# Third edge stage of a four-layer graph network: rows picked from the raw node features in two bfloat16 blocks, 176 columns, with ScalarE making 4 of 25 node blocks

## The reference, cut to what matters

```
q = x @ Wq + bq;  k = x @ Wk + bk;  v = x @ Wv + bv        # [3125, 64], 4 heads of 16
score = exp(clip(sum_over_16(k[src] * q[dst]) / 8, -5, 5))   # per edge and head
wv = segment_sum(v[src] * score, dst);  z = segment_sum(score, dst)
o = (wv / (z + 1)) @ Wo + bo;  h = x @ Wf + bf + o;  out = h + norm(h) * gamma + beta
```

## Time and profile before

| | us |
|---|---|
| median of 3 runs | 5953.28 (5952.83 to 5963.26) |
| span of the profiled execution | 5023.8 |
| time outside the span (5953.3 - 5023.8) | 929.5 |
| third edge stage, 3037 to about 3873 | 836 |
| first and second edge stage, about | 1000 and 1680 |

### The profile page before, as it was taken

One profiled execution on the slowest core, in us unless ns is written; L12 is line 12 of the kernel. 1 busy time (PEld: TensorE's weight loads), 2 busy tenths in 40 slices (PEclk: granted clock), 3 DMA queues, 4 the chain that ended last, 5 costly groups with the idle time before them and its releaser, 6 DMA issues. The chain is left out here.

```text
span 5023.8 us, 55747 instructions
## 1 busy us (share of the span) xinstructions
PE 3828.8 (76%) x16477; PEld 2687.1 (53%) x16477; DVE 4001.3 (80%) x5661; ACT 2076.3 (41%) x3728; POOL 3704.0 (74%) x3415
## 2 busy tenths in 40 slices
PE   1677777762999999999999947888883666677651
PEld 1344444432888888888888843333331443333321
DVE  3788888874899999999999856899996657677763
ACT  0577777751344444444444423444443322222221
POOL 6777777764788888888888637777776567777774
PEclk6899999985999999999999957899996778888875
DMA  8777887764788888888888643444443662222221
GB/s 304 261 274 277 283 282 281 281 213 141 281 326 316 320 322 317 325 314 328 316 320 323 250 93 111 131 131 131 132 129 99 240 248 66 72 68 72 66 62 44
DMA packets 359919, 1074.05 MB, mean 214 GB/s; under 512 B 101414, under 2 KB 124642, under 8 KB 315300
## 3 DMA queue, kind: packets, MB, share of 16 engines
q1 hardware_dynamic: 240788, 850.33, 44.9%
q0 software_dynamic: 103232, 158.19, 12.5%
q10 hardware_dynamic: 15696, 63.31, 3.1%
HBM read 677.98 MB, written 392.57 MB: 213 GB/s over the span
## 5 line engine op out<-in xcount | busy, mean ns | idle before, releaser
L1859 PE MATMUL COLS<-CF,XF 128*128 128x256 f32 x6272 | 1485.6, 380 | 6.2 <-DVE XF L1967 6.2
L1859 PEld LDWEIGHTS COLS<-CF,XF 128*128 128x128 f32 x6272 | 1135.0, 190 | 130.4 <-DVE XF L1967 6.6
L1135 ACT ACTIVATE OUT<-SC 128x576 f32<-128x576 f32 (+3 forms) x392 | 576.9, 1472 | 1082.2 <-DVE SC L1070 722.1
L1826 POOL DMA_INDIRECT G<-x_tab,SRC x784 | 835.7, 1066 | 229.1 <-issue 216.4
L1018 POOL DMA_INDIRECT G<-xl_tab,SRC x752 | 728.3, 969 | 229.2 <-issue 223.4
L1018 POOL DMA_INDIRECT G<-rel_tab,REL x672 | 641.5, 955 | 205.0 <-issue 205.0
L1018 POOL DMA_INDIRECT G<-kv_tab,SRC x640 | 628.6, 982 | 195.0 <-issue 193.5
L1444 PE MATMUL PICK<-HOT,KV 125*128 125x512 bf16 x2700 | 629.2, 397 | 132.4 <-ACT TURNED L1476 117.8
L1608 PE MATMUL MADE<-XM,W 128*128 128x512 f32 x896 | 484.6, 699 | 163.7 <-DVE XM L1696 163.6
L1444 PEld LDWEIGHTS PICK<-HOT,KV 125*128 125x128 bf16 x2700 | 272.2, 101 | 482.6 <-issue 179.6
L1262 PE MATMUL WK<-W,HT 128*128 128x256 f32 x1568 | 443.8, 409 | 0.0
(11 more groups left out here) (307 smaller groups left out, 6763.3 us busy)
## 6 DMA issues: line engine op xcount, KB each, us to landing
SHB<-ea9t SPq DMA_DIRECT2D x196, 1024.0 KB, 9.6
wkv_tab<-WKV SPq DMA_DIRECT2D x98, 1024.0 KB, 6.1
WKV<-wkv_tab SPq DMA_DIRECT2D x98, 1024.0 KB, 5.9
scan<-OUT SPq DMA_DIRECT2D x196, 288.0 KB
scan<-OUT ACTq DMA_DIRECT2D x98, 576.0 KB
rel_tab<-YS SPq DMA_DIRECT2D x50, 1024.0 KB, 12.6
RAW<-spread SPq DMA_DIRECT2D x196, 256.0 KB, 2.8
spread_q<-ZQ SPq DMA_DIRECT2D x98, 512.0 KB
```

The source lines that it names most:

```text
L1135: nc.scalar.activation(self.OUT[d][:, :, 0:WD], SC[b][:, 0:WD, 1:1 + C].rearrange("p r j -> p j r"), ACT.Copy).then_inc(self.copied_out, 1)
L1826: pool.indirect_dma_start(out=e.G[0][b][:, col, :], out_offset=None, in_=x1_tab, in_offset=bass.IndirectOffsetOnAxis(ap=SRC[:, at:at + 1], ...
L1859: nc.tensor.matmul(acc, XF[b][:, k, edges_], CF[:, k, :], start=(k == 0), stop=False)
```

## The change

Instead of the rows of `k` and `v`, the raw node features `x` are picked, and are projected after that.

- `X3` takes the place of `KV3`: two bfloat16 blocks of 128 columns instead of three. Block 0 holds the high and the middle part of the 64 features side by side, block 1 the low part and 64 zeros. PE makes 100 matmuls a batch instead of 150.
- The sum isn't transposed back but multiplied by `WKV2` (the weights of `k` and `v`, one above the other, so that the parts are added), with the biases first, in two halves of four columns (`project_half`).
- Chunks 8 to 95 each have 2 picked columns: 22 batches of four chunks, 176 columns instead of 144. POOL gathers 608 columns instead of 640.
- DVE makes 21 of the 25 blocks of `HOT` (in quarters of 6, 5, 5 and 5), in 462 compares instead of 450. ACT makes the other 4 in three parts, as relu(1 - |source - node|): an `Abs` for each block and a `Relu` for each part. These lie between `place` and `OUT` of the first three chunks of four; `take` lies in the fourth.
- The sources are loaded and narrowed one batch earlier, and ACT makes the first batch's 4 blocks before chunk 0.

```diff
+PERIOD = 4
+BATCHES = (NCH - PICK_FROM) // PERIOD
 def picks(t):
-    return 0 if t < PICK_FROM else (2, 1, 2, 1, 2)[(t - PICK_FROM) % 5]
+    return 2 if PICK_FROM <= t < PICK_FROM + PERIOD * BATCHES else 0
...
-                            act.wait_ge(m_copied, len(units))
-                            nc.scalar.activation(KV3[:, :, 0, :], TAB[:, :, 0:128], ACT.Copy).then_inc(kv_high, 1)
+                            nc.scalar.activation(X3[:, :, 0, 0:64], X[:, :, :], ACT.Copy).then_inc(x_high, 1)
...
+                            nc.gpsimd.memset(X3[:, :, 1, 64:128], 0.0).then_inc(blank, 1)
...
+                QUARTERS = [range(0, 6), range(6, 11), range(11, 16), range(16, 21)]
+                BY_ACT = [(21, 22), (23,), (24,)]
...
+                        def pick_rows(k, first, last):
+                            for piece in range(2):
+                                for half in range(2):
+                                    edges_ = slice(512 * half, 512 * half + 512)
+                                    ins = nc.tensor.matmul(PICK[:, edges_], X3[N, k, piece, :], HOT[N, k, edges_],
+                                                           start=(first and piece == 0), stop=(last and piece == 1))
+                            return ins
+                        def pick_by_act(i):
+                            wait(pe, act_compared, 3 * i + 3)
+                            wait(pe, taken, i)
+                            for k in range(21, K):
+                                ins = pick_rows(k, k == 21, False)
+                            ins.then_inc(act_read, 1)
...
+                        def project_half(i, h):
                             wait(pe, taken, i + 1)
-                            wait(pe, placed, 5 * i)
-                            for q in range(8):
-                                ins = nc.tensor.transpose(BACK[:, q * P:(q + 1) * P], TURNED[:, q * P:(q + 1) * P],
-                                                          IDENT[:, :])
+                            wait(pe, placed, 4 * (i - 1) + 2 * h + 2)
+                            nc.tensor.matmul(BACK[:, 512 * h:512 * h + 512], IDENT[:, :],
+                                             vec("bk", 2).unsqueeze(1).to_broadcast([P, 4, P]), start=True, stop=False)
+                            for q in range(4 * h, 4 * h + 4):
+                                ins = nc.tensor.matmul(BACK[:, q * P:(q + 1) * P], TURNED[:, q * P:(q + 1) * P],
+                                                       WKV2[:, :], start=False, stop=(q == 4 * h + 3))
                             ins.then_inc(turned_back, 1)
...
+                        def compare_by_act(i, part):
+                            ks = BY_ACT[part]
+                            if part == 0:
+                                wait(act, narrowed, i + 1)
+                                wait(act, act_read, i)
+                            wait(act, act_compared, 3 * i + part)
+                            for a, k in enumerate(ks):
+                                nc.scalar.activation(AWAY[N, a, :], ID16[i % 2][N, :], ACT.Abs,
+                                                     bias=MINUS_NODE[N, k - 21:k - 20]).then_inc(away, 1)
+                            wait(act, away, 4 * i + (2, 3, 4)[part])
+                            nc.scalar.activation(HOT[N, ks[0]:ks[-1] + 1, :], AWAY[N, 0:len(ks), :], ACT.Relu,
+                                                 bias=ONES[N, 0:1], scale=-1.0).then_inc(act_compared, 1)
...
-                            if t % 5 == 0 and 1 <= t // 5 <= BATCHES:
-                                take(t // 5 - 1)
+                            if t % PERIOD == 3 and t // PERIOD < BATCHES:
+                                take(t // PERIOD)
+                            elif t % PERIOD != 3 and t // PERIOD + 1 < BATCHES:
+                                compare_by_act(t // PERIOD + 1, t % PERIOD)
                             e.store_rows(act, t, n, b, t < 4)
```

More of the change, by code:

```diff
@@ L1414, in _ @@
                         load_sources(0)
+                        load_sources(1)
+                        for a in range(2):
+                            sp.dma_start(WKV2[64 * a:64 * a + 64, :], w64[:, W_COLS["Wk"][0]:W_COLS["Wv"][1]])\
+                              .then_inc(w_in, 16)
                         def step(t, n, b, first, last):
                             e.load_spread(sp, t, n, b, first)
-                            if t % 5 == 0 and t // 5 + 1 < BATCHES:
-                                load_sources(t // 5 + 1)
+                            if t % PERIOD == 0 and t // PERIOD + 2 < BATCHES:
+                                load_sources(t // PERIOD + 2)
                             if t >= 5:
@@ L1435, in _ @@
                     def _(pe):
-                        def pick(i, q):
[L1437 to L1446, removed]
+                        def pick_rows(k, first, last):
[5 more added lines that the diff above has]
+                            return ins
@@ new lines, in pick_by_act @@
+                        def pick_by_act(i):
[4 more added lines that the diff above has]
+                            ins.then_inc(act_read, 1)
+                        def pick(i, q):
+                            wait(pe, compared, 4 * i + q + 1)
+                            for k in QUARTERS[q]:
+                                ins = pick_rows(k, False, k == 20)
@@ L1460, in _ @@
                             if i >= 1:
-                                turn_back(i - 1)
-                            for q in range(2, 5):
-                                pick(i, q)
-                        turn_back(BATCHES - 1)
+                                project_half(i - 1, 0)
+                            pick(i, 2)
+                            pick(i, 3)
+                            if i >= 1:
+                                project_half(i - 1, 1)
+                        project_half(BATCHES - 1, 0)
+                        project_half(BATCHES - 1, 1)
                     @block.scalar
@@ L1486, in _ @@
                         narrow(0)
+                        narrow(1)
+                        wait(act, negated, 1)
+                        for part in range(3):
+                            compare_by_act(0, part)
                         wait(act, e.ready, e.N_READY)
@@ L1505, in _, with compare @@
                     def _(v):
[L1506 to L1507 removed]
+                        def compare(at, part):
+                            i, q = divmod(at, 4)
                             if i < BATCHES:
+                                ks = QUARTERS[q]
                                 wait(v, narrowed, i + 1)
[L1510 to L1511 removed]
+                                wait(v, read, 4 * (i - 1) + q + 1)
+                                for k in (ks[0:3], ks[3:])[part]:
                                     ins = nc.vector.tensor_scalar(HOT[N, k, :], ID16[i % 2][N, :], NODE_F[N, k:k + 1],
                                                                   None, ALU.is_equal)
[L1514 removed]
+                                if part == 1:
                                     ins.then_inc(compared, 1)
+                        nc.vector.tensor_scalar(MINUS_NODE[:, :], NODE_F[:, 21:25], -1.0, None, ALU.mult)\
+                          .then_inc(negated, 1)
                         e.constants(nc.vector)
[L1518 to L1519 removed]
+                        for at in range(2):
+                            compare(at, 0)
+                            compare(at, 1)
                         wait(v, e.ready, e.N_READY)
```

68 lines of the change are left out of this document (33 added, 35 removed).

## The result

The changed kernel took 5871.17 us (median of four, 5864.18 to 5931.81) against 5954.41 us of the kernel before on the same chip. That is 83 us less by the medians. The ratio of the runs is 0.9876, some 74 us, with a 95% interval from 0.9832 to 0.992. The forecast was -40 us, 5913 with a range of 5896 to 5945, so the sign was right, the size about half of what came, and the result lies outside the range.

A forecast was written before the change was run, and what follows sets the result against it. POOL's gathers were taken to bound the third edge stage. Gathers -39.1 us and `project` -1.1 us, all else zero, gave -40 us from 5953.3, so 5913 us, with a range of 5896 to 5945.

The forecast's parts named there:

- So the stage is as long as POOL's gathers: Third edge stage: 640 gathers at 1.287 us make 823.6 us, nearly the whole stage, with DVE second, close behind.
- I can't see what fills the 929.5 us.: Timed median outside the profiled span: 929.5 us, taken as unchanged; if all stretches in proportion, gain 47 us, time 5906.
- Gathers, -39.1 us at 1.287 each: POOL, third edge stage: 32 gathers fewer, from 823.6 to 784.5 us, -39.1; if all cost 1.287, -41.2.
- cost zero: PE, third edge stage: 27 us of work in a 31 us batch, so no cost to the time.
- A wait for `TURNED` before `PICK`: Sign for PE and ACT in the third edge stage: ACT's `TURNED` should not wait for `PICK`.
- the 25 named: DVE sign, third edge stage: less than 25 us idle before `T` in chunks 8 to 85.
- no new wait: Sign in the third edge stage: DVE gets no new wait of `MSG` for ACT.
- the 7.7: DVE's time for a third-stage chunk after the change: 7.6 + 0.12 = 7.7 us, level with POOL's 7.8.
- the sum: ACT's added work a batch, third edge stage: 4 x 1.04 + 2 x 1.04 + 1.9 = 8.1 us, taken to cost zero.
- DVE and ACT become the bound: Rival, third edge stage: 5929 or 5945 us; chance 0.17 for taking part of POOL's gain, 0.09 for nearly all.
- PE's clock falls: Rival, third edge stage: slow matmuls make PE the bound, typically +20 us, 5973; chance 0.08 together with ACT's queue.
- should keep their times: Sign: the first two, fourth and the rest of the third layer's phases stay unchanged in time.

The follow-up runs named there:

- e0: The kernel before, unchanged, run once more with a profile: 6002.97 us against 5993.91, ratio 1.0008.
- e1: The kernel before with 32 gathers fewer in the third edge stage (608 instead of 640), nothing else: 5915.84 us, -1.44% against the kernel before.
- e13: The kernel before with a 128 x 224 memset on POOL behind each third-stage gather: 5830.55 us, ratio 0.9731 to the kernel before; stage 948 us.
- e11: The changed kernel with a 128 x 224 memset on POOL behind each third-stage gather: 5782.33 us, ratio 0.9667 to the kernel before; stage 896 us.
- e2: The kernel before with only the two raw-row blocks and the projection, 640 gathers and 144 picked columns: 5978.01 us, -0.33% against the kernel before.
- e3: The changed kernel with a third piece in each block again, 150 pick matmuls a batch instead of 100: 6114.65 us, +1.86% against the kernel before.
- e9: The changed kernel with 20 pick matmuls a batch instead of 100, gathers as they were: 5777.3 us, -3.46% against the kernel before.
- e7: The changed kernel with its 608 third-stage gathers replaced by plain copies issued by SP: 5639.32 us, -5.99% against the kernel before.
- e16: The changed kernel with its 608 third-stage gathers replaced by plain copies issued by POOL: 5640.01 us, -6.09% against the kernel before.
- e14: The changed kernel with a 128 x 224 memset behind each gather of the first, third and fourth edge stage: 5592.35 us, ratio 0.9331 to the kernel before.
- e8: The changed kernel with a 128 x 96 memset on POOL behind each third-stage gather: 5905.63 us, ratio 0.9831 to the kernel before; stage 987 us.
- e6: The changed kernel with each of its 608 third-stage gathers replaced by two POOL memsets: 5820.83 us, -3.08% against the kernel before.

## Why the prediction was wrong

- **"So the stage is as long as POOL's gathers": the step that failed.** It was read well from the profile at hand, but the timed executions don't run so. POOL waits for `SC` 304.5 us in e0 and 245.2 us after, where the forecast had 1.5 and named 5 as the mark of being wrong. The sign to follow was in the forecast: "I can't see what fills the 929.5 us." It was held constant, when that rest is over 20 times the effect sought. In those executions PE's work, or its counts, reach ACT late, in the wait shown by 13 us, ACT stands in `take` or `place`, DVE waits for `MSG` or `T`, the ring fills, and POOL stops.
- **Gathers, -39.1 us at 1.287 each.** The count was right; 32 fewer were worth 94 us of stage (e1), 2.9 each, since they take holds away too. Where POOL's pace is the bound it is 52 (e13 to e11). That the sign came right is in part luck: fewer gathers helped, mostly for a reason that the forecast didn't have.
- **PE, "cost zero".** Wrong: its work counts when it is held (e2, e3, e9). A wait for `TURNED` before `PICK` was named as the mark of a wrong forecast, and it is 257.9 us in 20 cases. The clock is 0.79 in the stage in e0 and after, just under the 0.8 named and under the first profile's 0.87; being alike on both sides, it isn't what the change gained.
- **DVE.** `T` has 15.7 us of idle time, under the 25 named, but not because POOL is level with DVE: before `MSG` it waits 178.0 us for ACT, where "no new wait" was the mark. Its chunk is 7.4 to 7.9 us where nothing is held (e7, e16), as the 7.7 said.
- **ACT.** `Abs` is 1.14 us and the single `Relu` 1.15, the double one 2.0, where the sum had 1.04 and 1.9. A batch is 4.57 + 4.30 = 8.9 us (88 and 66 instructions by their means, 22 batches), not 8.1. The estimate by the Trainium skill ("ScalarE: Activation LUTs", Rules for kernel authors) was 8.9, and the trace agrees with it. Neither decided anything.
- **Rivals.** "DVE and ACT become the bound" and "PE's clock falls" both didn't come. PE did become what is waited for, but by another mechanism, and on both sides of the change.
- **The four stages.** They "should keep their times": the first is 14 us shorter between the profiles of e0 and after, the rest behind the third 16. No edit touches them; between the chips of these runs the kernel before itself goes from 5954 to 6015.

## What to carry to other kernels

Hold the span of the profile against the timed median first; where they differ by more than the effect sought, get a profile of that condition before costing anything. Where an engine's last record and the start of its waiter lie 10 us apart, look at what a third engine does in between. And where runs of indirect gathers stand beside a busy PE, try a short pause behind each: it gained 2.7% in one stage of the kernel before (e13), and with the change, in three stages, 6.7% (e14).

## What the runs showed of the hardware

- Indirect gathers of 128 rows at 1.25 us one behind the other hold PE back. ACT sees its counts up to 16 us behind its last record (e0), or PE starts one matmul in 2 to 3 us (e2). As many rows of 512 bytes by plain copies of POOL (0.585 us each) or of SP don't do it. At 1.48 us a gather the holds are nearly gone in the changed kernel (15.6 us of idle time before `TURNED`, e11) and less than half are left in the kernel before (184.7 us of ACT's two waits in e13, 467.5 in e0); at 1.36 most are left (216.9, e8). The first profile had the same gathers at 1.287 us and no hold, so a second condition belongs to it, which no run here shows. What holds PE inside is open too. The Trainium skill ("NOTIFIC — the notification-queue block", Overflow: three behaviours, one of which stalls the engine) says that this block's own pipeline holds its producers back rather than lose a record. All executions from e0 on came with records, so no run here shows whether one without them has the holds.
- A memset on POOL slows DVE's 16-bit compares from 0.48 to 0.88 us on the mean (e6; 0.82 without one record of 30 us), at 128 x 224 to 0.56. The Trainium skill ("SBUF — State Buffer", SBUF: two separate sides) has GpSimd share one pair of ports with VectorE's instructions in a two-port mode, by turns for a whole instruction. The trace of e6 agrees: 266 of the 462 compares took 0.5 to 0.6 us and 186 took 1.2 to 1.3. Whether these compares are in that mode no run here shows.
